# A graph network kernel on one core: POOL makes every fifth block of high-digit one-hots in the count of the sources' degrees

## The reference

```python
ones_e = jnp.ones(src.shape[0], dtype=emb_table.dtype)
deg_out = jax.ops.segment_sum(ones_e, src, num_segments=n)
norm_src = jax.lax.rsqrt(jnp.maximum(deg_out, 1.0))
```

## Time and profile before

| | |
|---|---|
| time, median of 3 runs | 10004.24 us (9991.14 to 10006.8) |
| profiled execution: span from first to last instruction | 9988.2 us |
| profiled execution: time on the device beside the span | not given; the median lies 16 us above the span |
| the count: first one-hot, last matmul | 16.6 us, 347 us |
| DVE, L597 x200 | 133.5 us busy, 686 ns each |
| DVE, L601 x120 | 116.2 us busy, 968 ns each |
| ACT, L621 x640 | 178.9 us busy, 362 ns each |
| ACT, L624 x80 | 75.8 us busy, 948 ns each |
| PE, L636 x1600 | 146.4 us busy, 283 ns each |

### The profile page before, as it was taken

One profiled execution on the slowest core, in us unless ns is written; L12 is line 12 of the kernel. 1 busy time (PEld: TensorE's weight loads), 2 busy tenths in 40 slices (PEclk: granted clock), 3 DMA queues, 4 the chain that ended last, 5 costly groups with the idle time before them and its releaser, 6 DMA issues.

```text
span 9988.2 us, 178573 instructions
## 1 busy us (share of the span) xinstructions
PE 7824.2 (78%) x39865; PEld 6121.3 (61%) x39865; DVE 7971.0 (80%) x24833; ACT 5963.0 (60%) x18344; POOL 6961.9 (70%) x7476
## 2 busy tenths in 40 slices
PE   4444555555799999898889989888888888848887
PEld 4333444444477777777677777666666666636665
DVE  7787556555878887999967768788888888899999
ACT  6777777777877774111100006688888888846665
POOL 0466777777078887777678877566666666649995
PEclk6555555555899999999999999855565565557876
DMA  2222222222588888887766662322222222210000
GB/s 52 54 48 48 53 53 53 53 53 53 189 253 239 243 238 267 287 289 280 247 250 224 224 214 61 81 49 49 49 50 49 49 50 49 50 28 1 1 1 27
DMA packets 530133, 1151.52 MB, mean 115 GB/s; under 512 B 147134, under 2 KB 398210, under 8 KB 508750
## 3 DMA queue, kind: packets, MB, share of 16 engines
q0 software_dynamic: 241872, 477.23, 19.9%
q10 hardware_dynamic: 22752, 517.02, 13.2%
q1 hardware_dynamic: 264478, 145.85, 5.5%
HBM read 886.72 MB, written 259.31 MB: 115 GB/s over the span
## 4 chain that ended last, share of the span: by engine, by line
DVE 24%; POOL 23%; PE 22%; issue 14%; ACT 11%; DVEq 3%; DMA 2%; SPq 1%; ACTq 0%; POOLq 0%
POOL onehot L2185 9%; PE bank L1413 7%; POOL step_data L1743 7%; POOL step_data L1449 4%; PE bank_tile L2042 3%; POOL gather_ring L1449 3%; ACT onehot L1028 2%; DVE keys L1099 2%; DVE keys L1108 2%; ACT onehot L1026 2%; PE bank L1039 2%; DVE keys L1471 2%; DVE arena L1072 2%; PE bank_tile L2052 2%; DVE keys L2022 2%
## 5 line engine op out<-in xcount | busy, mean ns | idle before, releaser
L1014 POOL DMA_INDIRECT gather_ring<-mean_rows,step_data x1660 | 1596.1, 961 | 784.3 <-PE bank L1039 288.2
L1039 PE MATMUL bank<-gather_ring,onehot 128*128 128x130 f32 x3320 | 1042.1, 460 | 1053.0 <-DVE arena L1072 724.8
L1413 PE MATMUL bank<-arena 128*128 128x384 bf16 x8526 | 1628.5, 330 | 30.4 <-DMA arena<-split_out 26.9
L1413 PE MATMUL bank<-arena,keys 128*128 128x384 bf16 x8526 | 1623.5, 330 | 11.8 <-DMA arena<-split_im 11.8
L1039 PEld LDWEIGHTS bank<-gather_ring,onehot 128*128 128x128 f32 x3320 | 805.8, 306 | 1279.1 <-issue 851.6
L1413 PEld LDWEIGHTS bank<-arena 128*128 128x128 bf16 x8526 | 1178.9, 139 | 289.8 <-issue 47.5
L1413 PEld LDWEIGHTS bank<-arena,keys 128*128 128x128 bf16 x8526 | 1177.4, 138 | 270.5 <-issue 24.7
L1743 POOL DMA_INDIRECT step_data<-next_rows,window_idx x896 | 1045.9, 1167 | 351.1 <-issue 263.9
L1449 POOL DMA_INDIRECT step_data<-hidden,window_idx x888 | 1060.9, 1195 | 293.9 <-issue 265.9
L1966 POOL DMA_INDIRECT gather_ring<-attention_rows,step_data x834 | 786.8, 943 | 435.5 <-PE bank_tile L2042 228.6
L1966 POOL DMA_INDIRECT keys<-attention_rows,step_data x826 | 779.3, 943 | 388.0 <-PE bank_tile L2042 227.1
(11 more groups left out here) (350 smaller groups left out, 20302.8 us busy)
## 6 DMA issues: line engine op xcount, KB each, us to landing
keys<-count_rows ACTq DMA_DIRECT2D x50, 3136.0 KB
arena<-count_rows ACTq DMA_DIRECT2D x50, 3136.0 KB
count_rows<-arena ACTq DMA_DIRECT2D x26, 3136.0 KB
count_rows<-keys ACTq DMA_DIRECT2D x26, 3136.0 KB
gather_ring<-mean_rows,step_data POOLq DMA_INDIRECT x1660, 2.5
step_data<-next_rows,window_idx POOLq DMA_INDIRECT x896
step_data<-hidden,window_idx POOLq DMA_INDIRECT x888
gather_ring<-attention_rows,step_data POOLq DMA_INDIRECT x834
```

The source lines that it names most:

```text
L1014: e.indirect_dma_start(ring_at(rings.slot(name, i), SUM_COLS, SUMS - 1), None, rows, bass.IndirectOffsetOnAxis(src_idx[:, i:i + 1], 0), bo ...
L1039: e.matmul(pass_bank[i % N_SUM_BANKS][:, 0:SUMS], onehot[:, i % STEP_SLOTS, :], ring_at(rings.slot(name, i), SUM_COLS, SUMS), start=True, ...
L1413: m = e.matmul(pass_bank[n % 2][:, 0:SPLIT_COLS], counts[t % 2][:, :, h], split[:, h, :], start=(h == 0), stop=(h == NODE_TILES - 1))
```

## The change

The function `far` is now written with period ten but picks the same groups (0, 2, 5, 7 of ten). A new predicate `aside` picks i % 5 == 4. In these groups DVE no longer makes the high one-hots; POOL does, with eight `tensor_scalar` instructions of 125 x 98, bf16 in and out, compared with the digit as a scalar of each partition in f32, each raising a new semaphore. POOL's part is a generator too, and it is put into POOL's queue around the gathers.

```diff
     def far(i):
 
-        return i % 5 in (0, 2)
+        return i % 10 in (0, 2, 5, 7)
+
+    def aside(i):
+
+        return i % 5 == 4
...
@@ hist_vector
-            if not far(i):
+            if not far(i) and not aside(i):
...
@@ hist_tensor
-            e.wait_ge(hist_near if far(i) else hist_high, FARS[i + 1] if far(i) else i + 1 - FARS[i + 1])
+            if far(i):
+                e.wait_ge(hist_near, FARS[i + 1])
+            elif aside(i):
+                e.wait_ge(hist_side, HIST_COLS * ASIDES[i + 1])
+            else:
+                e.wait_ge(hist_high, i + 1 - FARS[i + 1] - ASIDES[i + 1])
...
+    def hist_gpsimd(e):
+        for i in range(HIST_GROUPS):
+            if aside(i):
+                if i >= HIST_SLOTS:
+                    e.wait_ge(hist_summed, i - HIST_SLOTS + 1)
+                for c in range(HIST_COLS):
+                    at = i * HIST_COLS + c
+                    e.tensor_scalar(high_store[:, i % HIST_SLOTS, c, :], iota_half[0:LOAD_PARTS, 0:NODE_TILES],
+                                    high_digit[:, at:at + 1], None, ALU.is_equal).then_inc(hist_side)
+            yield
...
@@ prep_pool_program
+        e.wait_ge(prep_vector.sem, mark["digits"])
+        counting = hist_gpsimd(e)
+        some_of(counting, HIST_FIRST)
         e.wait_ge(prep_vector.sem, mark["bound_idx"])
         e.indirect_dma_start(bound_row, None, dst_wide, bass.IndirectOffsetOnAxis(bound_row_idx, 0),
                              bounds_check=LOAD_PARTS - 1, oob_is_err=False).then_inc(bounds_landed, 16)
+        some_of(counting, HIST_BETWEEN)
         e.wait_ge(prep_vector.sem, mark["row_idx"])
         for g in range(STEP_GROUPS):
             s = g % 2
             if g >= 2:
                 e.wait_ge(prep_vector.sem, mark["edges_read", g - 2])
+                some_of(counting, HIST_BESIDE)
             e.indirect_dma_start(edge_rows_sb[s], None, a["edge_rows"],
                                  bass.IndirectOffsetOnAxis(row_idx[:, g:g + 1], 0), bounds_check=EDGE_ROWS - 1,
                                  oob_is_err=False).then_inc(edges_landed[s], 16)
+        for _ in counting:
+            pass
```

More of the change, by code:

```diff
@@ L475, in program @@
     hist_low = sem("source_low_onehots")
+    hist_side = sem("source_high_onehots_by_pool")
     hist_far = sem("source_high_distances")
@@ L585, in far @@
     def far(i):
-        return i % 5 in (0, 2)
+        return i % 10 in (0, 2, 5, 7)
+    def aside(i):
+        return i % 5 == 4
     FARS = list(itertools.accumulate((far(i) for i in range(HIST_GROUPS)), initial=0))
+    ASIDES = list(itertools.accumulate((aside(i) for i in range(HIST_GROUPS)), initial=0))
     def hist_vector(e):
```

## The result

The changed kernel takes 10077.66 us (median of 4 runs, 10073.1 to 10081.76), the kernel before 10000.3 us (4 runs, 9991.14 to 10006.8): ratio 1.0078, 95% interval 1.0063 to 1.0092. It is slower, as forecast; 77 us more where 51 were forecast, inside the range. The profiled spans are 10071.4 and 9988.2 us, 83 us apart; the 6 us between 77 and 83 are less than the spread of single runs (9 us after, 16 us before).

The account below looks back on a forecast made before the run. ACT's two groups in five, 6.25 us, were taken to bound the late count. +42 us there and +9 in the edge row steps made +51, added to 10004.2 for 10055 us; range 10006 to 10088.

Parts of the forecast that it names:

- DVE is not on the path; ACT's two groups in five are: Count after the edge row steps: ACT's two groups set 6.25 us for five; DVE sits idle 0.49 us.
- The loop L + 1.7: Four-slot ring: POOL's time for its group, plus 1.7 us for PE's two groups and handovers, before POOL restarts.
- A POOL instruction, 0.55 us: Each of POOL's eight small instructions takes 0.55 us uncontended, 4.4 us a group; bounds 0.44 and 0.58.
- Contention: one POOL instruction per DVE instruction, L = 6.0: Late count: beside busy DVE, POOL's group takes 6.0 us, five groups 7.7 instead of 6.25; +42 us.
- The upper bound of that term: Late count: at most about +62 us, with POOL's group at 6.7 us and all eight instructions beside DVE's.
- rivals 3 and 4: Full exclusion between DVE and POOL, 10105 us, chance 0.06; a dearer POOL instruction, 10080 or more, chance 0.09.
- The edge row steps, +9 us: Count's 13 early steps: waits for POOL's groups outweigh DVE's saved high one-hots, +9 us in sum.
- All carried on: End of the count: all engines wait there, so the whole +51 us moves the rest of the program.
- The 16 us: Whole kernel: the profiled span lies 16 us under the median of three runs, 10004.2, used as base.
- The rival that takes the Trainium skill by its word: Late count: one instruction blocks the other throughout, five groups 9.2 us, about +100 with the steps; chance 0.06.
- my 7.7: Late count: forecast time in us for five groups with POOL's part, instead of 6.25.

Follow-up runs that it names:

- e2: Changed kernel, with POOL's eight instructions as memsets that only write; the count ends at 341.2 us instead of 347.2 in the kernel before.
- e4: Kernel before, with eight ring slots instead of four; ratio 0.9995, the count ends at 346.1 us.
- e7: Kernel before, with eight slots and ACT making every second high one-hot to group 52, then three in eight; ratio 0.9993, count ends at 332.3 us.
- e1: Changed kernel, with DVE waiting for its last one-hot to end before starting the next; five groups 8.3 us, count ends at 417.8 us.
- e8: Changed kernel, with DVE's low one-hots as memsets that read nothing; POOL's group takes 5.59 us, five groups 7.3.
- e3: Changed kernel, with eight ring slots instead of four; five groups 7.1 us, count ends at 373.8 us, ratio to the kernel before 1.003.
- e5: Changed kernel, with POOL taking every fifth group only from group 54 on; five groups 8.87 us, count ends at 422.3 us.
- e9: Changed kernel, with one POOL subtract of 125 x 784 per group instead of eight comparisons; count ends at 343.8 us.

## Why the prediction was right, and what it had wrong

- *DVE is not on the path; ACT's two groups in five are.* Right: e2 relieves DVE and keeps 6.24 us; e4 relieves the ring and keeps 6.25; e7 relieves ACT and gets 1.18 a group.
- *The loop L + 1.7.* Right: 7.11 + 1.74 = 8.85, e1 and e8 with other L, and e3, where the 1.74 fall away.
- *A POOL instruction, 0.55 us.* It is 0.50 beside idle DVE. With the 0.58 of 128 elements that is 2.5 ns an element, not the 0.91 of the iota (the types differ too).
- *Contention: one POOL instruction per DVE instruction, L = 6.0.* That POOL's reads are held up by DVE's is shown (e2, e8); the size was short: one per two, L = 7.11, 8.86 - 6.25 = 2.61 us more for each of 29 fives, 76 us instead of 42. This is the term that was mis-sized. The earlier trace rows could not tell one from two: the POOL instruction of 787 ns began at 8905.92, in the last 0.05 us before the second of five L2196 (8905.97), and the third (8906.23) is the one that is lengthened. It let the second pass, but whether it stood waiting during the first can't be read there.
- *The upper bound of that term*, 62 us (L = 6.7), rested on the same one-per-one and lies under the 76 that came. With it the sum would have ended at 10004 + 62 + 9 = 10075 us, and 10077.66 came. That the range held the time is in part luck: its upper end (10080, and 10088 with the near parts of rivals 3 and 4) had room that came from other rivals.
- *The edge row steps, +9 us.* The sum is near (+9.3 at their end), but only 8.1 of it lie between the first and the last step; they begin 1.1 us later, where the prediction had nothing (e5, without POOL up to there: 0.5 later). Of the parts, the steps behind groups 14 and 29 took 8.4 us (forecast 8.55), those behind 24 and 39 8.9 and 9.0 (8.55). Group 44 cost no such wait, since POOL had no gather left to do before it and started it a step earlier than I counted.
- *All carried on.* 85 us at the end of the count, 83 in the span.
- *The 16 us* I added from span to median were the spread of the runs: of the profiled run after, 1.7 us lie outside its span.
- The rival that takes the Trainium skill by its word ("SBUF — State Buffer", "Who interferes with whom": the later instruction blocks for the other's whole length) forecast +100 us and 9.2 us for five. That price was too low by the prediction's own loop: DVE's six instructions (4.2 us), POOL's eight (4.4) and the 1.7 make 10.3 us. The measured 8.86 lies between this and my 7.7. That POOL's read waits for the whole rest of a DVE instruction agrees with every group shown here, and e2 agrees with the exception for POOL instructions that only write. Which of the two started first by the record does not decide alone: in e8 the POOL instruction of 260.22 waits for the DVE one of 260.38. In the other direction the whole instruction doesn't hold for small ones: DVE loses 0.06 to 0.07 us in the group shown to a POOL instruction of 0.52, though 1.3 us to the one of e9. The turn that POOL loses to DVE's queued instruction is in the runs alone.

## What to carry to other kernels

Work moved off an engine that has slack wins nothing (only the steps, where DVE had none, could give 6 us here), and the receiver's latency enters every ring that it joins: work out (latency + the consumer's part) against the present period before moving anything. Small POOL instructions that read SBUF, beside back-to-back DVE instructions with two SBUF inputs, took 1.29 to 1.78 us each here, up to two DVE instructions' time, although they take 0.52 alone. If it must be POOL, one large instruction for each block is the form to try first (e9: 1.85 us for the whole group), with the price that DVE's next instruction waits 1.3 us; e9 makes differences and not one-hots, so it shows the time of such a kernel and is not one. What helped the count here was to give the full engine less (ACT three in eight instead of two in five): 15 us of it, for no POOL at all, though too little to be measured in the whole kernel.

## What the runs showed of the hardware that was not expected

TensorE's granted clock in the edge row steps was 0.50 in the kernel before and 0.88 after, with PE busy 32.07 of 74 us and 32.87 of 83; in the part behind it 0.50 and 0.57. What raised it is not shown. The time doesn't hang on it in the places read here: PE's two groups take 1.50 us before and 1.51 after, and DVE waits about 1.05 us for the transposes in most steps of both.
